# State-space block and routed feed-forward on one core: constants on another queue, loads reordered at the start, four more weight tiles resident before the last router logits

## Chip, core and metric

The kernel runs on one core of a Trainium2 chip, in one launch. The metric is the device time of that launch in microseconds. The engines are named as in the profile: PE (TensorE, matmul), PEld (its weight load), DVE (VectorE), ACT (ScalarE), POOL (GpSimd) and SP (SyncE, which here only issues DMAs). All arrays are float32.

## What is computed

Four batches of 1024 tokens with 1024 features go through two layers. The first is a selective state-space layer over a context of 512 features; the second is a feed-forward layer whose two experts per batch are picked by a router that looks at the whole normalised batch.

```python
def ssm(hidden, z, in_proj_w, conv_w, conv_b, x_proj_w, dt_proj_w, dt_proj_b, A_log, D):
    x = einsum('ed,bld->bel', in_proj_w, hidden)            # 512 -> 1024 channels
    u = silu(causal_conv4(x, conv_w) + conv_b)
    dt_lo, Bm, Cm = split(einsum('ke,bel->bkl', x_proj_w, u), (32, 16, 16))
    delta = softplus(einsum('er,brl->bel', dt_proj_w, dt_lo) + dt_proj_b)
    A = -exp(A_log)
    # for each token t:  state = state * exp(delta_t * A) + (delta_t * u_t) * B_t ;  y_t = state . C_t
    y = (scan(...) + D * u) * silu(z)
    return swapaxes(y, 1, 2)

x = x + ssm(ctx, layernorm(x), ...)

def ffn(x, switch_w, switch_b, w1, b1, w2, b2, w3, b3):      # x: layernorm(x)
    logits = x.reshape(b, -1) @ switch_w.T + switch_b        # 1024*1024 values against 8 experts
    gate, top = top_k(softmax(logits), 2)
    h = gelu(x_heads @ w1[top].T + b1[top])                  # 16 heads of 64
    o = sum_k gate_k * (h @ w2[top].T + b2[top])
    return (x + o) @ w3.T + b3

x = x + ffn(layernorm(x), ...)
```

## The kernel before

The work is written out by hand for each engine, with semaphores between them. The scan is cut into 64 blocks, `g` = 0 to 63: 4 batches, two halves of 512 tokens (`TH`), and 8 blocks of 128 channels (`J`). One block is one *step* and has 8 *slots*; a slot is a pair of the 16 states, for which ACT makes the decay `dA`, DVE the product with B (L1343) and two scans (L1370), POOL the product with C (L791), and PE the sum over states by transposing into `yT` (L854). The class `Schedule` says in which slot every other piece of work runs; each engine walks the same list `PLAN.slots[b][t]` in order. While batch `b` is scanned, the feed-forward layer of batch `b-1` runs between the scans. The last feed-forward has nothing beside it; it is the list of `b = 4`, made by `tail`.

**The start.** Before slot 0 each engine has a piece written out by hand.
- SP issues, in this order: the context (`ctxs`), the first block of in_proj weights, the convolution's `cw` and `cb`, then for `k` = 0 to 7 the weights of block `k` (into `Bb`, from `k` = 1 on) and the row block `k` of x (512 KB, into `Cb`), then the second half of the context (`first_ctx`, into `Bb[8:12]`), two more weight blocks (`win`) and `xz`. Then it waits for PE.
- ACT issues eleven small DMAs (L1029): five for the state-space layer (`Av`, `xpw`, two for `dtw`, `Dv`) and six for the feed-forward layer (`b1c` and `b2c` twice each, `b3c`, `swb`). All eleven count on one semaphore, `const_loaded`. Only behind them stands ACT's first work: for block `G` a copy of the last columns (L1040) and the first tap of the convolution (L1041), and, after DVE's three taps (L1218), Silu (L1056), which makes `u`.
- PE computes in_proj for `G` = 0 to 7 (L861, 8 matmuls a block in the trace), and behind block `G >= 2` the part of x_proj for block `G - 2` (L837). The first x_proj part waits for `const_loaded`, and PE runs its queue in order. Then come block 8, the last part of x_proj, the first delta (L846) and block 9.
- ACT's `split_rows` copies the result of x_proj out. SP stores the B and C rows to `bc_d` in DRAM and loads them back, spread over all partitions, one slot's pair `q` at a time into `Bb` and `Cb` (L542, 512 KB each). Ahead of the first of these it waits until in_proj of block 9 is done (`xin_done`), since `first_ctx` still lies in `Bb[8:12]`.
- DVE's block `G` is three taps and then the statistics of row block `G` (L1254 to L1260). After block 9's taps it makes the first product with B.

**The tail.** The router's logits of a batch's second half are 32 tiles of weights (`sw`, 512 KB each, four row blocks of 8) against normalised rows (L986). In the tail the tiles go through a ring of 19 places (`ring_t`): 3 in `sww`, 4 in `w3h`, 8 in `Cb` and 4 in `Bb`. The first 7 are loaded in slot 0 of the tail, in the last microseconds of the scan; the 12 in `Cb` and `Bb` after the last scan has let go of these; the last 13 are refills. Four row blocks for later (`Bb<-x_scratch`) are issued between the 12 and the 13. Behind the last logit come the router (L1306 to L1441), the experts and the output product (L1007, 16 output tiles), which occupy PE to the end.

`u` is a ring of 10 places (`UR`); block `g` uses place `g % 10`, so no block is written into it after block 63.

## Time and profile before

| | us |
|---|---|
| median of 3 runs | 2579.28 |
| lowest, highest | 2577.56, 2580.72 |
| the profiled execution | 2580.0 |
| its span, first to last instruction | 2578.2 |

| engine | busy us | share of the span |
|---|---|---|
| DVE | 2238.0 | 87% |
| PE | 1940.0 | 75% |
| ACT | 1537.1 | 60% |
| POOL | 1446.6 | 56% |

How to read it: the shares are averages over three different stretches. Between about 90 and 2350 us the scans run and DVE has almost no gap. Before 90 us stands the hand-written start, after 2350 us the last feed-forward. The page's line of 40 slices (64 us each) shows DVE at 3 tenths in the first slice and at 5, 2, 1 and 0 in the last four. The chain that ended last has 32% of the span on PE, 26% on DVE and 23% in issue.

### The profile page before, as it was taken

What the parts mean: (1) busy time and instruction counts of PE and PEld (TensorE: products, weight loads), DVE (VectorE), ACT (ScalarE), POOL (GpSimd) and SP (SyncE); (2) the same over time, 40 slices, a digit from 0 to 9 for tenths busy, and PEclk for the clock granted to TensorE, in tenths of its full rate; (3) what the DMA queues carried; (4) which work ended last, traced back from release to release, by engine and by line L of the source; (5) the groups of instructions that cost most, each with busy time, mean ns of one, the idle gap of its engine ahead of it and who ended that gap; (6) DMA issues with size and microseconds to landing.
All of it is one profiled execution on the core that took longest, in us unless ns stands there. A gap on an engine that the chain in (4) does not pass through costs nothing.

```text
span 2578.2 us, 30156 instructions
## 1 busy us (share of the span) xinstructions
PE 1940.0 (75%) x9488; PEld 1093.3 (42%) x9488; DVE 2238.0 (87%) x2928; ACT 1537.1 (60%) x2221; POOL 1446.6 (56%) x990
## 2 busy tenths in 40 slices
PE   5565656666776898898675888799685797896799
PEld 2344444344443454454443455344453354453244
DVE  3899999999999899998999989998999999995210
ACT  1566556555667657854666757855576858852400
POOL 0477666666775556665775656565775666663000
PEclk8767776887887899998787999999787999997899
DMA  5411252545552364566452364466460274566511
GB/s 150 164 33 57 83 172 76 178 147 176 194 174 100 98 216 147 158 207 200 170 206 74 116 229 139 141 215 197 159 235 21 72 238 147 175 193 226 211 57 66
DMA packets 201617, 387.84 MB, mean 150 GB/s; under 512 B 31697, under 2 KB 97233, under 8 KB 201458
## 3 DMA queue, kind: packets, MB, share of 16 engines
q1 hardware_dynamic: 194992, 385.43, 44.8%
q10 hardware_dynamic: 6466, 0.48, 0.2%
q8 instruction: 76, 1.25, 0.2%
q14 instruction: 83, 0.68, 0.1%
HBM read 351.78 MB, written 34.08 MB: 150 GB/s over the span
## 4 chain that ended last, share of the span: by engine, by line
PE 32%; DVE 26%; issue 23%; ACT 9%; POOL 6%; DMA 2%; SPq 1%; DVEq 1%; ACTq 1%; POOLq 0%
DVE h L1370 12%; PE dense L1007 10%; PE dense L854 7%; DVE dense L1343 5%; POOL h L791 5%; PE dense L825 4%; ACT dA L1127 3%; DVE u L1218 3%; PE dense L837 2%; PE dense L928 1%; PE dense L938 1%; ACT L1084 1%; PE dense L846 1%; DVE szT L1287 1%; PE dense L861 1%
## 5 line engine op out<-in xcount | busy, mean ns | idle before, releaser
L791 POOL TENSOR_TENSOR h<-h,Cb 128x1024 f32<-128x1024 f32 x512 | 1208.5, 2360 | 456.3 <-DVE h L1370 432.7
L1127 ACT ACTIVATE dA<-delta,Av 128x512 f32<-128x512 f32 x1024 | 702.6, 717 | 519.9 <-DVE h L1370 517.4
L854 PE MATMUL dense<-ident,h 128*128 128x128 f32 x4096 | 643.3, 313 | 289.6 <-POOL h L791 287.5
L854 PEld LDWEIGHTS dense<-ident,h 128*128 128x128 f32 x4096 | 550.9, 162 | 465.5 <-POOL h L791 376.8
L1370 DVE TENSOR_TENSOR_SCAN h<-dA,state,dense 128x512 f32<-128x512 f32 x512 | 627.6, 1263 | 41.3 <-PE dense L854 22.4
L1343 DVE TENSOR_TENSOR dense<-dense,Bb 128x512 f32<-128x512 f32 x1024 | 652.9, 683 | 5.0 <-DMA Cb<-bc_scratch 2.9
L1370 DVE TENSOR_TENSOR_SCAN h<-dA,dense 128x512 f32<-128x512 f32 x512 | 597.3, 1202 | 17.6 <-ACT dA L1127 9.9
L1007 PE MATMUL dense<-w3h,xT 128*128 128x512 f32 x832 | 390.5, 603 | 0.0
L785 POOL COPY state<-h 128x2 f32<-128x2 f32 x256 | 48.0, 187 | 373.3 <-DVE h L1370 371.8
L846 PE MATMUL dense<-dtaug,dtw 33*128 33x512 f32 x128 | 103.0, 896 | 180.0 <-DVE u L1218 178.2
L825 PE MATMUL dense<-ctxs,win 128*128 128x512 f32 x432 | 224.4, 667 | 1.9 <-ACT dtw L1063 1.0
L1007 PEld LDWEIGHTS dense<-w3h,xT 128*128 128x128 f32 x832 | 149.1, 194 | 129.6 <-issue 129.6
L1218 DVE SCALAR_TENSOR_TENSOR u<-dense,cw,u 128x511 f32<-128x511 f32 (+2 forms) x192 | 140.3, 731 | 35.8 <-ACT u L1041 28.0
L1084 ACT ACT_TABLE_LOAD x113 | 145.0, 1283 | 2.0
L1329 DVE TENSOR_TENSOR res<-dense,res 128x512 f32<-128x512 f32 x64 | 43.8, 684 | 111.3 <-PE dense L1007 110.9
L825 PEld LDWEIGHTS dense<-ctxs,win 128*128 128x128 f32 x432 | 90.9, 221 | 111.4 <-issue 111.4
L986 PE MATMUL dense<-sww,row 128*32 128x256 f32 x1336 | 110.9, 418 | 14.3 <-ACT row L1160 14.3
L1080 ACT COPY dense<-du_s 128x512 f32<-128x512 f32 x64 | 37.6, 588 | 134.2 <-DVE dense L1343 134.2
L846 PEld LDWEIGHTS dense<-dtaug,dtw 33*128 33x128 f32 x128 | 25.6, 249 | 211.3 <-issue 211.3
L938 PE MATMUL dense<-hs,w2s 128*64 128x512 f32 x224 | 71.3, 707 | 41.4 <-ACT hs L1192 40.6
L748 POOL TENSOR_TENSOR du_s<-delta,u 128x512 f32<-128x512 f32 x64 | 81.6, 1275 | 5.7 <-DVE delta L1248 5.7
L778 POOL TENSOR_TENSOR xt<-szT,xt 128x512 f32<-128x512 f32 x64 | 81.7, 1277 | 3.0 <-DVE szT L1287 3.0
(141 smaller groups left out, 1846.0 us busy)
## 6 DMA issues: line engine op xcount, KB each, us to landing
sww<-in_sw SPq DMA_DIRECT2D x170, 512.0 KB, 4.4
Bb<-bc_scratch SPq DMA_DIRECT2D x64, 512.0 KB, 4.6
Cb<-bc_scratch SPq DMA_DIRECT2D x64, 512.0 KB, 5.8
w3h<-in_sw SPq DMA_DIRECT2D x56, 512.0 KB, 7.6
w3h<-in_w3T SPq DMA_DIRECT2D x52, 512.0 KB, 5.1
row<-x_scratch SPq DMA_DIRECT2D x42, 512.0 KB, 4.8
xz<-in_x SPq DMA_DIRECT2D x64, 256.0 KB, 5.0
xt<-in_x SPq DMA_DIRECT2D x64, 256.0 KB, 4.4
```

What stands on the lines that cost most here:

```text
L791: e.tensor_tensor(h[:, s:s + 2, :], h[:, s:s + 2, :], Cb[:, 2 * q:2 * q + 2, :], ALU.mult).then_inc(prod_done, 1)
L825: mm = e.matmul(dense[:, bank, :], win[:, par, k, :], ctxs[:, k, :], start=(k == 0), stop=(k == DK - 1))
L846: e.matmul(dense[:, S, :], dtw[0:DR + 1, j * P:(j + 1) * P], dtaug[:], start=True, stop=True) \
L854: mm = e.matmul(yT[:, k, :], h[:, 2 * (q % RH) + i, k * P:(k + 1) * P], ident[:], is_transpose=True, start=False, stop=(q == PAIRS - 1 and ...
L938: mm = e.matmul(dense[HD * i:HD * i + HD, bank, :], w2s[:], hs_of(b, hp)[:, i, :], start=True, stop=True)
L986: mm = e.matmul(dense[32 * n:32 * n + 32, F2, 0:32 * E], rows[:, lo:lo + 32], weights[:, :, 32 * n:32 * n + 32], start=first, stop=(k % TB ...
L1007: mm = e.matmul(dense[:, bank, :], xT_of(b, uu)[:, d, k * P:(k + 1) * P], w3[:, d, :], start=False, stop=(d == J - 1), skip_group_check=True)
L1084: e.preload_act_table_set("natural_log_exp_and_others")
L1127: e.activation(dst, delta[:, st % 2, :], ACT.Exp, scale=Av[:, j * N + n:j * N + n + 1]).then_inc(dA_done, 1)
L1218: i = e.scalar_tensor_tensor(out=u[:, G % UR, s:T], in0=dense[:, bank, 0:T - s], scalar=cw[:, j, k:k + 1], in1=u[:, G % UR, s:T], op0=ALU. ...
L1343: e.tensor_tensor(duB[:, n % 2, :], du[:], Bb[:, n, :], ALU.mult).then_inc(duB_done, 1)
L1370: e.tensor_tensor_scan(h[:, 2 * (q % RH) + n % 2, :], decay, inflow, state[:, j * N + n:j * N + n + 1] if th else 0.0, ALU.mult, ALU.add) \
```

## The change

Four edits:
1. The six feed-forward constants leave ACT's queue. SP issues them behind `xz`, on a semaphore of their own, `ffn_const_loaded`. `const_loaded` counts five. DVE waits for the new semaphore at each `route1`, PE once, ahead of the first output tile of batch 1.
2. On SP the loads of in_proj weights go two places ahead of the row blocks of x.
3. The wait for block 9's in_proj stands ahead of the pair `q = 4` of the B/C loads, not ahead of `q = 0`.
4. The tail's ring has 23 places: four new ones at its head, in places 4 to 9 and 0 to 1 of `u`. They are loaded in slots 112, 114, 116 and 118 of the last batch, each behind waits for the blocks that used that place. 9 refills are left.

```diff
-RING_A, RING_B, RING_T = 8, 3, 19
+RING_A, RING_B, RING_U, RING_T = 8, 3, 4, 23
...
     def tail(self, rows):
         b = NB
-        for i in range(RING_T):
-            self.add(b, 0 if i < RING_B + 4 else 5, "sw_load", TB + i // SWL, i % SWL)
+        for i in range(RING_U):
+            self.add(b - 1, 112 + 2 * i, "sw_ahead", i)
+        for i in range(RING_U, RING_T):
+            self.add(b, 0 if i < RING_U + RING_B + 4 else 5, "sw_load", TB + i // SWL, i % SWL)
...
-        ring_t = [*ring_b, *sw_tiles(w3h[:], 4), *sw_tiles(Cb[:], 8), *sw_tiles(Bb[:, 8:16, :], 4)]
+        ring_t = [*sw_tiles(u[:, 4:UR, :], 3), *sw_tiles(u[:, 0:2, :], 1), *ring_b, *sw_tiles(w3h[:], 4), *sw_tiles(Cb[:], 8), *sw_tiles(Bb[:, 8:16, :], 4)]
...
-        CONSTS = 11
+        CONSTS, FFN_CONSTS = 5, 6
...
-            for k in range(J):
-                if k:
+            for k in range(J + 2):
+                if 0 < k < J:
                     e.dma_start(first_win[k], w_inT[k]).then_inc(first_win_loaded[k], 16)
+                if k < 2:
+                    continue
+                k -= 2
                 e.dma_start(first_rows[k], x[0:1, k * P:(k + 1) * P, :].rearrange("o p d -> p (o d)")) \
...
             load_xz(0, 0, 0)
+            with nc.allow_non_contiguous_dma(reason="small weights, once"):
+                for dst, src in (
+                    (b1c[0:HD], b1.rearrange("e f -> f e")),
...
+                    (swb[:], sw_b.partition_broadcast(P)),
+                ):
+                    e.dma_start(dst, src).then_inc(ffn_const_loaded, 16)
             e.wait_ge(xin_done, 1 + J + 1)
             load_ctx(0, 1)
...
             e.wait_ge(bc_stored, 1 + 16)
-            e.wait_ge(xin_done, 1 + 1 + AHEAD)
             for q in range(PAIRS):
+                if q == J // 2:
+                    e.wait_ge(xin_done, 1 + 1 + AHEAD)
                 e.wait_ge(first_row_read, 1 + q + 1)
                 load_bc(0, q)
...
+                    elif what == "sw_ahead":
+                        last = ALL - AHEAD + 2 * a[0] + 1
+                        e.wait_ge(uD_done, 1 + last + 1)
+                        e.wait_ge(du_s_done, 1 + last + 1)
+                        dst, done, _ = sw_tile(NB, TB, a[0])
+                        e.dma_start(dst, sw[TB * P:(TB + 1) * P, a[0]]).then_inc(done, 16)
...
                         if part == 0:
+                            if b == 1 and uu == 0 and dh == 0 and k == 0:
+                                e.wait_ge(ffn_const_loaded, 1 + 16 * FFN_CONSTS)
...
                     (Dv[:], D.rearrange("(j p) -> p j", p=P)),
-                    (b1c[0:HD], b1.rearrange("e f -> f e")),
-                    (b1c[HD:P], b1.rearrange("e f -> f e")),
-                    (b2c[0:HD], b2.rearrange("e d -> d e")),
-                    (b2c[HD:P], b2.rearrange("e d -> d e")),
-                    (b3c[:], b3.rearrange("(j p) -> p j", p=P)),
-                    (swb[:], sw_b.partition_broadcast(P)),
...
                 e.wait_ge(lg_done, 1 + b)
+                e.wait_ge(ffn_const_loaded, 1 + 16 * FFN_CONSTS)
```

ACT's queue at the start, before. Each row is an instruction with what it writes and reads; in brackets the semaphores it waits for.

```order
L1029 DMA Dv<-in_D 128x8x1
L1029 DMA b1c<-in_b 64x8x1 x2
L1029 DMA b2c<-in_b 64x8x1 x2
L1029 DMA b3c<-in_b 128x8x1
L1029 DMA swb<-in_sw_b 128x8
L1040 ACT_TABLE_LOAD [waits u_done,edge_done,xin_done]
L1040 COPY halo<-dense 128x3 [waits conv_loaded]
```

The same place after the change:

```order
L1050 DMA xpw<-in_x_projT 128x8x64
L1050 DMA dtw<-in_dt_projT 32x1024
L1050 DMA dtw<-in_dt_b 1x1024
L1050 DMA Dv<-in_D 128x8x1
L1061 ACT_TABLE_LOAD [waits u_done,edge_done,xin_done]
L1061 COPY halo<-dense 128x3 [waits conv_loaded]
```

The table load, which waits for block 0's in_proj, now stands right behind `Dv`.

SP's queue at the start, before, from `xz` to the first pairs of B and C:

```order
L546 DMA xz<-in_x 128x512
L537 DMA ctxs<-in_ctxT 128x4x512 [waits xin_done]
L566 DMA bc_scratch<-dtw 32x512 [waits evac0]
L542 DMA Bb<-bc_scratch 128x1024 [waits first_row_read,xin_done,bc_stored]
L542 DMA Cb<-bc_scratch 128x1024
L542 DMA Bb<-bc_scratch 128x1024 [waits first_row_read]
```

And after, to pair 4 (two rows for each of the pairs 1 to 3 left out):

```order
L549 DMA xz<-in_x 128x512
L578 DMA b1c<-in_b 64x8x1 x2
L578 DMA b2c<-in_b 64x8x1 x2
L578 DMA b3c<-in_b 128x8x1
L578 DMA swb<-in_sw_b 128x8
L540 DMA ctxs<-in_ctxT 128x4x512 [waits xin_done]
L582 DMA bc_scratch<-dtw 32x512 [waits evac0]
L545 DMA Bb<-bc_scratch 128x1024 [waits first_row_read,bc_stored]
L545 DMA Cb<-bc_scratch 128x1024
...
L545 DMA Bb<-bc_scratch 128x1024 [waits first_row_read,xin_done]
```

The six constants stand between `xz` and the second context load, and the wait for `xin_done` moved from the first pair to the fifth.

SP's queue in the tail, before:

```order
L588 DMA Bb<-x_scratch 128x1024 [waits x1_stored,duB_s_done,duB_done] x4
L669 DMA sww<-in_sw 128x1024 [waits sw_used] x3
L669 DMA w3h<-in_sw 128x1024 [waits sw_used] x4
L669 DMA Cb<-in_sw 128x1024 [waits sw_used] x6
L686 DMA w3h<-in_w3T 128x1024 [waits sw_used]
```

And after:

```order
L605 DMA Bb<-x_scratch 128x1024 [waits x1_stored,duB_s_done,duB_done] x4
L694 DMA u<-in_sw 128x1024 [waits sw_used] x4
L694 DMA sww<-in_sw 128x1024 [waits sw_used] x3
L694 DMA w3h<-in_sw 128x1024 [waits sw_used] x2
L711 DMA w3h<-in_w3T 128x1024 [waits sw_used]
```

The 13 refills have become 9, and the first four of them go into `u`.

## Rows read from the trace of the kernel before

**Rows 1.** The page, part 1: busy us, share of the span, instructions.
```profile
PE 1940.0 (75%) x9488; PEld 1093.3 (42%) x9488; DVE 2238.0 (87%) x2928; ACT 1537.1 (60%) x2221; POOL 1446.6 (56%) x990
```

**Rows 2.** Chain that ended at 110 us: start, us, what.
```profile
23.54 18.74 DMA swb<-in_sw_b
...
82.83 6.35 DMA Cb<-bc_scratch
```

**Rows 3.** Timeline of the start: start, us, engine, line, operation [idle before <-releaser].
```profile
14.81 2.85 ACTq L1029 DMA_DIRECT2D b1c<-in_b  x2
...
20.70 0.16 POOL L722 MEMSET cw<- 128x72 f32 x1 [10.01 <-DMA cb<-in_conv_b]
...
23.54 7.81 ACTq L1029 DMA_DIRECT2D swb<-in_sw_b  x1
...
30.15 1.20 SPq L546 DMA_DIRECT2D xz<-in_x  x1
31.52 1.28 ACT L1040 ACT_TABLE_LOAD   x1 [31.52 <-issue]
```

**Rows 4.** Timeline of PE and its weight loads at the start.
```profile
16.98 13.49 PE L861 MATMUL dense<-ctxs,Bb 128*128 128x512 f32 x24 [16.98 <-DMA Bb<-in_w_inT]
...
23.20 0.43 PEld L861 LDWEIGHTS dense<-ctxs,Bb 128*128 128x128 f32 x2 [0.63 <-DMA Bb<-in_w_inT]
...
42.32 1.97 PE L837 MATMUL dense<-u,xpw 128*64 128x512 f32 x2 [11.86 <-DMA swb<-in_sw_b]
...
49.12 1.07 PE L837 MATMUL dense<-u,xpw 128*64 128x512 f32 x2
...
69.52 3.70 PE L861 MATMUL dense<-Bb,win 128*128 128x512 f32 x8
```

**Rows 5.** Timeline of DVE at the start: taps, and the first product with B.
```profile
33.69 2.32 DVE L1218 SCALAR_TENSOR_TENSOR u<-dense,cw,u 128x511 f32<-128x511 f32 x3 [21.55 <-ACT u L1041]
...
37.74 2.31 DVE L1218 SCALAR_TENSOR_TENSOR u<-dense,cw,u 128x511 f32<-128x511 f32 x3
...
84.00 2.31 DVE L1218 SCALAR_TENSOR_TENSOR u<-dense,cw,u 128x511 f32<-128x511 f32 x3 [3.92 <-ACT u L1050]
89.20 1.30 DVE L1343 TENSOR_TENSOR dense<-dense,Bb 128x512 f32<-128x512 f32 x2 [2.88 <-DMA Cb<-bc_scratch]
```

**Rows 6.** DMA queues (q1 SP's, q10 ACT's), 0 to 22 us: packets, MB, share.
```profile
q1 hardware_dynamic: 3053, 2.20, 39.2%
q10 hardware_dynamic: 3690, 0.47, 17.4%
```

**Rows 7.** The same two queues, 0 to 36 us.
```profile
q1 hardware_dynamic: 4908, 7.36, 62.2%
q10 hardware_dynamic: 5494, 0.48, 13.8%
```

**Rows 8.** SP's store of B and C, timeline; landing times of their DMAs.
```profile
75.82 0.34 SPq L566 DMA_DIRECT2D bc_scratch<-dtw  x1
...
DMA to landing us min/median/max: 1.6/10.0/15.0
```

**Rows 9.** Stretches: from:to us, busy (count) by engine, PEclk, DMA share, GB/s.
```profile
2288.00:2320.00 32.00, 30.68 (x173) 16.63 (x174) 31.79 (x38) 18.69 (x27) 21.48 (x11) 1.00 0.65 200
2374.00:2390.00 16.00, 10.18 (x100) 3.67 (x96) 0.00 (x0) 2.20 (x4) 0.00 (x0) 0.79 1.03 409
```

**Rows 10.** Timeline of PE in the tail's logits.
```profile
2367.39 2.79 PE L986 MATMUL dense<-sww,row 128*32 128x256 f32 x24 [13.87 <-ACT row L1160]
...
2376.52 0.64 PE L986 MATMUL dense<-Cb,row 128*32 128x256 f32 x8 [0.64 <-DMA Cb<-in_sw]
...
2380.36 1.08 PE L986 MATMUL dense<-Cb,row 128*32 128x256 f32 x8 [0.20 <-DMA Cb<-in_sw]
...
2398.03 1.97 PE L915 MATMUL dense<-ident,ctxs 128*128 128x128 f32 x8
...
2407.22 0.64 PE L986 MATMUL dense<-Cb,ctxs 128*32 128x256 f32 x8 [0.60 <-DMA Cb<-in_sw]
```

More of the change, by code:

```diff
@@ L358, in build @@
         const_loaded = sem("const_loaded")
+        ffn_const_loaded = sem("ffn_const_loaded")
         first_win_loaded = [sem(f"first_win_loaded{G}") for G in range(J)]
@@ L562, in _ @@
             load_xz(0, 0, 0)
+            with nc.allow_non_contiguous_dma(reason="small weights, once"):
+                for dst, src in (
+                    (b1c[0:HD], b1.rearrange("e f -> f e")),
+                    (b1c[HD:P], b1.rearrange("e f -> f e")),
+                    (b2c[0:HD], b2.rearrange("e d -> d e")),
+                    (b2c[HD:P], b2.rearrange("e d -> d e")),
+                    (b3c[:], b3.rearrange("(j p) -> p j", p=P)),
+                    (swb[:], sw_b.partition_broadcast(P)),
+                ):
+                    e.dma_start(dst, src).then_inc(ffn_const_loaded, 16)
             e.wait_ge(xin_done, 1 + J + 1)
@@ L649, in slot @@
                         m = SWL * (k % TB) + i
-                        ring = RING_B if k < TB else RING_A if b < NB else RING_T
+                        if b == NB:
+                            m -= RING_U
+                        ring = RING_B if k < TB else RING_A if b < NB else RING_T - RING_U
                         if m >= ring:
-                            e.wait_ge(sw_used, 1 + sw_index(b, k, i) - ring + 1)
+                            e.wait_ge(sw_used, 1 + sw_index(b, k, i) - (RING_T if b == NB else ring) + 1)
                         elif k < TB:
```

## The prediction

> **What bounds the kernel now.** The page first: DVE is busy 87% of the span [rows 1], but that average says nothing of the two ends, where the change sits. So I read the start and the tail each by chain, timeline and DMA views.
>
> *The start.* The chain that ended at 110 us [rows 2] has one large piece: 18.74 us up to the landing of `swb`, a feed-forward constant that nobody needs before batch 1. The timeline of ACT says what else it does [rows 3]: the six feed-forward DMAs occupy ACT's queue from 14.81 to 31.35 us, and only then comes its first table load. PE [rows 4] has three in_proj blocks done at 16.98 + 13.49 = 30.47 us, then stands 11.86 us for `swb`, comes back slower (x_proj 1.97 us against 1.07 later) and ends block 8 at 73.22. DVE's first taps start at 33.69, and its first product at 89.20 waits 2.88 us for C [rows 5]. Two things are therefore late at once: ACT, which frees DVE, and the constants, which free PE.
>
> *The scans.* DVE is busy 31.79 of 32.00 us near the end of them [rows 9]. What the start gives arrives whole at the tail.
>
> *The tail.* DMA moves 409 GB/s at a share of 1.03 from 2374 to 2390 us, while PE is busy 10.18 of 16 us [rows 9]; ahead of a tile that takes 0.64 us it stands 0.64 us for the transfer, and so still at 2407.22 [rows 10]. The logits are bound by the volume of weights. Behind them runs a chain in which nothing can overtake.
>
> **The change, part by part.**
>
> *Constants off ACT.* After it ACT's next instruction is the table load that waits for in_proj of block 0. That block ends when block 1's weights are loaded, at 23.20 [rows 4]; `cw` and `cb` are there at 20.70 [rows 3]. The load starts at 23.2 instead of 31.52, 8.3 us earlier, and DVE's first taps at 33.69 - 8.3 = 25.4.
>
> PE's x_proj part 0 now wants five constants. By their shapes these are 3 x 1024 packets and under 200 for `dtw`, some 3,270; ACT's queue had moved 3,690 at 22 us [rows 6]. They are there 8 us before 30.47. It wants `u` of block 0 too: a whole DVE cycle is 37.74 - 33.69 = 4.05 us [rows 5], so 25.4 + 4.05 = 29.5 at the latest. PE goes on at 30.47 without a gap and without the slow restart. Then x_proj part 0 and block 3 take 1.07 + 3.70 less 0.1 of overlap, 4.7 us; from x_proj part 1 to the end of block 8 it was 73.22 - 49.12 = 24.1. End of block 8: 30.47 + 4.7 + 24.1 = 59.2 instead of 73.22, **14.0 us earlier**. Is DVE late instead? It reaches block 7's taps at 25.4 + 7 x 4.05 = 53.8; PE ends block 7 at 59.2 less 3.70 and two x_proj parts, 53.6, and ACT's step comes after that. PE stays the bound, with less than 1 us between them. All that follows block 8 up to the taps of block 9 is a fixed sequence: these end at 72.3 instead of 86.3.
>
> *Constants on SP.* SP is free at 31.35 [rows 3]. Even if the six issues take their 16.5 us again it is free at 47.9. Next on its queue is the second context load, released by block 7's in_proj at 53.6, then the store of B and C at 75.82 - 14.0 = 61.8 [rows 8]. Cost nothing; the cover is 5.7 us for the one and 13.9 for the other. The new waits (DVE at each `route1`, PE once) come hundreds of us later and are met: nothing, or some tens of ns each.
>
> *Weights before row blocks.* Block 1 waited 0.63 us ahead of its weight load, most of it the usual step from block to block: a gain of 0.1 at most, below nothing not, since row block 0 is wanted by DVE only at 25.4 + 2.3 = 27.7. The context, three weight blocks and that row block are 2.4 MB, and SP's queue had 2.20 MB over at 22 us; after that a row block and a weight block (0.79 MB) take 2.1 us at (7.36 - 2.20) MB in 14 us [rows 6, 7], against DVE's 4.05. Counted as 0.
>
> *B and C earlier.* The store is issued at 61.8; 1.6 us is the shortest landing of this stretch [rows 8], and the store goes into an idle queue: 63.4. The first C load is issued 0.4 us later and took 6.35 [rows 2]: 70.2. DVE's taps end at 72.3, so the C wait is gone and the conv is last: first product at **72.3 instead of 89.20, 16.9 us**. Without this edit the loads would begin behind block 9, as before, and the gain would stay at 14.0; it pays 2.9. Pair 4's wait ends with block 9, about 68.4; the four pairs before it are 4.2 MB, 10 us at 409 GB/s, so DMA has work until 73.6. Bounds: a landing of 10.0 us, the median [rows 8], gives 73.8 and 15.4 in all, one of 15.0 gives 78.8 and 10.4. I take 6.35, the same transfer into the same empty queues, and 13 for the low end.
>
> *Four tiles ahead.* A tile is 524,288 bytes, 1.28 us at 409 GB/s; four fewer in the bound stretch: **5.1 us**. The refills are released by tiles 0 to 8, which PE has done long before. The ahead loads go into 2288 to 2320 us, where DMA runs at 200 GB/s and share 0.65 [rows 9]: 2.1 MB more make 266. Nothing there waits for a load, so I cost them at nothing; without that cover they could cost up to 5.1. The other bound is PE at its low clock: a tile then takes 1.08 us, 1.01 net, and a turn of a row block 1.9 [rows 10]. Tile 30 would start at 2367.39 + 30 x 1.01 + 3 x 1.9 = 2403.4 instead of 2402.1 by DMA, and the last pieces cost another 1.3: a gain of 2.5. I take 5.1, since PE keeps up at 1.28 us a tile at either clock; above, 5.5.
>
> The rows speak against a rule here. Tiles come every 1.28 us, because transfers overlap. The Trainium skill (DMA: Bandwidth & Descriptors, the table of fixed and variable time ahead of "Queues, rings and completion order") puts about 2.0 us fixed on every DMA beside bytes / 436e9; by it four tiles would be worth 4 x 3.2 = 12.8 us. The trace does not agree.
>
> *Sum.* 16.9 + 5.1 = 22.0 us. The profiled execution took 2580.0 (1.8 outside its span), 0.7 above the median; a shift is the same for both: 2558.0 for such an execution, 2579.28 - 22.0 = **2557.3** for the median.
>
> **The rivals.**
> 1. *The start pays less*: B and C, or the five constants, land later than counted. For it: landings of 10 to 15 us exist in this stretch. Against it: those were queued behind others. With 13 at the start: 2561.2.
> 2. *The tail pays nothing or half*: the ahead loads push the steps' own, or PE's clock stays low. 2562.4 with nothing, 2559.9 with 2.5.
> 3. *The tiles pay more than volume*, each with its own latency, 1.6 + 1.28 = 2.9 us, 11.5 for four: 2550.9. Only if they went one at a time, which 409 GB/s excludes. The skill's fixed cost named above would be this case.
> 4. *PE still waits* behind a constant that lands late for another reason, and ACT's release buys nothing: 2.9 + 5.1 = 8.0, 2571.3.
> 5. *Slower: the six constants block SP.* Their issue stalls on SP, and behind it stand the context load and the store of B and C. Each us that SP is free after 61.8 + 2.1 = 63.9 costs one; from 85.9 on, 54.5 us for the six, the whole gain is gone; with 60 us it is 2584.8. Against it: they took 16.5 us on ACT, and in the time that they waited their packets moved one for one with SP's (1,804 and 1,855 between 22 and 36 us [rows 6, 7]). Behind x they have no such neighbour: 3,200 packets at the 562 per us of 10 to 22 us are 5.7 us. The one-for-one is what the Trainium skill says (the same page, "Queues, rings and completion order": each engine takes turns between queues packet by packet); by that rule the trace agrees, and this rival is the weaker for it.
>
> **How the numbers follow.** Chances: forecast 0.69, first rival 0.13, second 0.10, third 0.01, fourth 0.03, fifth 0.02, and 0.02 that both ends fail and the time stays. The range takes in the first two rivals and the bounds: low 2579.3 - 17.1 - 5.5 = 2556.7, less 1.7 for the spread of the runs shown, 2555.0; high 2579.3 - 13 - 2.5 = 2563.8. A measurement of this kernel can tell 0.2%, 5.2 us, from no change: faster 0.96, same 0.02, slower 0.02.
>
> **What the profile after would show.** ACT's first table load near 23.2 and DVE's first taps near 25.4; no gap in PE between block 2 and x_proj part 0, and both parts of it near 1.07; block 8 ending near 59.2; DVE's first product near 72.3 with ACT or its own taps, not C, ahead of it; SP's six issues over before 53.6. In the tail `u<-in_sw` loads between 2270 and 2300, 409 GB/s again in the logits, and from their first to their last 5.1 us less. Wrong would be: a DMA wait ahead of x_proj part 0, pair 0 landing after 72.3, a DVE gap where the ahead loads go, or PE busy through the logits.

## The result and the profile after

| | before | changed |
|---|---|---|
| median us (6 runs each, side by side) | 2579.20 | 2560.52 |
| lowest, highest | 2577.56, 2580.72 | 2559.50, 2563.02 |
| ratio, 95% interval | | 0.9929 [0.9917, 0.9942] |
| the profiled execution, its span | 2580.0, 2578.2 | 2559.85, 2557.8 |

18.7 us faster, where 22.0 were forecast and the range allowed 15.5 to 24.3. I cut both traces at five landmarks to see where the time came from:

| stretch, us | before | changed | gain | forecast |
|---|---|---|---|---|
| start of span to the first product with B | 89.20 | 72.47 | 16.7 | 16.9 |
| to the end of the last scan | 2259.87 | 2260.61 | -0.7 | 0 |
| to the first router logit of the tail | 18.32 | 18.56 | -0.2 | 0 |
| first to last logit | 42.06 | 37.44 | 4.6 | 5.1 |
| to the end | 168.75 | 168.72 | 0.0 | 0 |

The gains sum to 20.4 us of span. Outside the span the changed kernel takes 0.2 us more (2.05 instead of 1.8). The medians are 1.5 us closer together than the two profiled executions, of which the one before lies 0.8 above its median and the one after 0.7 below.

**The start.** Timeline of the changed kernel, ACT and SP, as [rows 3] (start, us, engine, line, operation, in brackets idle before and its releaser; a q is the engine's DMA issuing):

```profile
29.93 1.78 SPq L578 DMA_DIRECT2D b1c<-in_b  x2
31.76 7.06 SPq L578 DMA_DIRECT2D b2c<-in_b  x2
38.86 1.53 SPq L578 DMA_DIRECT2D b3c<-in_b  x1
40.43 0.58 SPq L578 DMA_DIRECT2D swb<-in_sw_b  x1
53.99 0.38 SPq L540 DMA_DIRECT2D ctxs<-in_ctxT  x1
62.06 0.34 SPq L582 DMA_DIRECT2D bc_scratch<-dtw  x1
63.70 0.34 SPq L545 DMA_DIRECT2D Bb<-bc_scratch  x1
...
24.00 1.28 ACT L1061 ACT_TABLE_LOAD   x1 [24.00 <-PE dense L886]
```

ACT's table load now waits for PE, not for its own issues. SP takes 11.1 us for the six constants and is free 13 us before the next thing is due. PE and DVE, as [rows 4, 5]:

```profile
17.48 13.32 PE L886 MATMUL dense<-ctxs,Bb 128*128 128x512 f32 x24 [17.48 <-DMA Bb<-in_w_inT]
30.72 1.07 PE L862 MATMUL dense<-u,xpw 128*64 128x512 f32 x2
...
55.75 3.70 PE L886 MATMUL dense<-Bb,win 128*128 128x512 f32 x8
63.20 5.40 PE L886 MATMUL dense<-Bb,win 128*128 128x512 f32 x8
...
26.17 2.31 DVE L1239 SCALAR_TENSOR_TENSOR u<-dense,cw,u 128x511 f32<-128x511 f32 x3 [13.77 <-ACT u L1062]
70.24 2.32 DVE L1239 SCALAR_TENSOR_TENSOR u<-dense,cw,u 128x511 f32<-128x511 f32 x3 [3.92 <-ACT u L1071]
72.47 1.29 DVE L1364 TENSOR_TENSOR dense<-dense,Bb 128x512 f32<-128x512 f32 x2
```

The 11.86 us that PE stood for `swb` are gone and x_proj part 0 takes 1.07 us. Block 8 ends at 55.75 + 3.70 = 59.45. The first product has no bracket: C was there. The page's part 3 gives the queues (packets, MB, share):

```profile
q10 hardware_dynamic: 3170, 0.47, 0.1%
```

3170 packets are what ACT's five constants alone make; the estimate by shapes was 3,270.

**The tail.** SP's ahead loads:

```profile
2272.15 0.33 SPq L669 DMA_DIRECT2D u<-in_sw  x1
2280.03 0.40 SPq L669 DMA_DIRECT2D u<-in_sw  x1
2286.67 0.39 SPq L669 DMA_DIRECT2D u<-in_sw  x1
2292.74 0.45 SPq L669 DMA_DIRECT2D u<-in_sw  x1
```

Two stretches, columns as in [rows 9]:

```profile
2271.00:2303.00 32.00, 30.23 (x167) 15.87 (x166) 31.79 (x37) 18.96 (x27) 22.24 (x11) 1.00 0.83 277
2374.00:2390.00 16.00, 12.36 (x86) 4.20 (x84) 0.81 (x2) 5.02 (x7) 0.00 (x0) 0.55 0.70 278
```

The first is the stretch of [rows 9] moved with the scans: 277 GB/s instead of 200 (266 forecast), and DVE's 31.79 us of 32 are the same. From 2360 to 2376 us, in the logits, DMA moved 409 GB/s as before. The second stretch catches the end of the logits, where the last transfers run out; its granted clock of 0.55 means that PE ran nearly all of it at 1.2 GHz. PE's rows there, as [rows 10]. L1011 is the tiles, eight matmuls each; L940 x8 is a *turn*, eight transposes of a normalised row block between two groups of tiles:

```profile
2351.64 3.26 PE L1011 MATMUL dense<-u,row 128*32 128x256 f32 x32 [14.12 <-ACT row L1181]
...
2373.29 1.94 PE L940 MATMUL dense<-ident,ctxs 128*128 128x128 f32 x8 [2.04 <-ACT xT L1202]
...
2385.52 1.08 PE L1011 MATMUL dense<-w3h,ctxs 128*32 128x256 f32 x8 [0.19 <-DMA w3h<-in_sw]
2386.53 1.97 PE L940 MATMUL dense<-ident,ctxs 128*128 128x128 f32 x8
2388.43 0.65 PE L1011 MATMUL dense<-w3h,ctxs 128*32 128x256 f32 x8
```

The tile at 2385.52 is the last but one, and still waits for its transfer. Its start lies 21.7 us before the same tile's 2407.22 [rows 10], more than the 20.4 that remain at the end. So the transfers gave more than the sum shows, and PE took some back behind them: tile and turn cost 1.08 and 1.97 us here, where the kernel before had 0.64 and 1.09 in the same place.

### The profile page after: what moved, and what is told of

It reads as the page before. It is cut to its first block, busy times and chain, and to the rows that moved or that the text cites. A ratio compares the mean times of both kernels' runs of the same rounds, so it can differ in the third digit from the quotient of the medians.

```text
span 2557.8 us, 30169 instructions
## 1 busy us (share of the span) xinstructions
PE 1942.7 (76%) x9488; PEld 1096.3 (43%) x9488; DVE 2238.3 (88%) x2928; ACT 1537.2 (60%) x2221; POOL 1445.2 (57%) x990
## 3 DMA queue, kind: packets, MB, share of 16 engines
q10 hardware_dynamic: 3170, 0.47, 0.1%
## 4 chain that ended last, share of the span: by engine, by line
PE 35%; DVE 26%; issue 22%; ACT 9%; POOL 5%; DMA 2%; DVEq 1%; SPq 0%; ACTq 0%; POOLq 0%
DVE h L1391 12%; PE dense L1034 11%; PE dense L879 7%; DVE dense L1364 5%; POOL h L816 5%; PE dense L850 4%; ACT dA L1148 3%; DVE u L1239 3%; PE dense L862 2%; PE dense L963 2%; PE dense L953 2%; PE dense L886 2%; PE dense L1011 1%; ACT L1105 1%; DVE szT L1308 1%
## 5 line engine op out<-in xcount | busy, mean ns | idle before, releaser
L879 PE MATMUL dense<-ident,h 128*128 128x128 f32 x4096 | 647.4, 314 | 282.4 <-POOL h L816 280.1
L879 PEld LDWEIGHTS dense<-ident,h 128*128 128x128 f32 x4096 | 554.1, 163 | 459.1 <-POOL h L816 368.5
L1391 DVE TENSOR_TENSOR_SCAN h<-dA,dense 128x512 f32<-128x512 f32 x512 | 597.7, 1204 | 17.5 <-ACT dA L1148 9.8
L850 PE MATMUL dense<-ctxs,win 128*128 128x512 f32 x432 | 223.4, 665 | 1.9 <-ACT dtw L1084 1.0
L1239 DVE SCALAR_TENSOR_TENSOR u<-dense,cw,u 128x511 f32<-128x511 f32 (+2 forms) x192 | 140.6, 732 | 21.7 <-ACT u L1062 13.8
L850 PEld LDWEIGHTS dense<-ctxs,win 128*128 128x128 f32 x432 | 90.4, 220 | 110.8 <-issue 110.8
L1011 PE MATMUL dense<-sww,row 128*32 128x256 f32 x1336 | 109.8, 415 | 0.4 <-ACT row L1181 0.4
L963 PE MATMUL dense<-hs,w2s 128*64 128x512 f32 x224 | 72.3, 717 | 41.4 <-ACT hs L1213 40.6
```

The lines of the kernel that those rows point to most:

```text
L850: mm = e.matmul(dense[:, bank, :], win[:, par, k, :], ctxs[:, k, :], start=(k == 0), stop=(k == DK - 1))
L879: mm = e.matmul(yT[:, k, :], h[:, 2 * (q % RH) + i, k * P:(k + 1) * P], ident[:], is_transpose=True, start=False, stop=(q == PAIRS - 1 and ...
L963: mm = e.matmul(dense[HD * i:HD * i + HD, bank, :], w2s[:], hs_of(b, hp)[:, i, :], start=True, stop=True)
L1011: mm = e.matmul(dense[32 * n:32 * n + 32, F2, 0:32 * E], rows[:, lo:lo + 32], weights[:, :, 32 * n:32 * n + 32], start=first, stop=(k % TB ...
L1239: i = e.scalar_tensor_tensor(out=u[:, G % UR, s:T], in0=dense[:, bank, 0:T - s], scalar=cw[:, j, k:k + 1], in1=u[:, G % UR, s:T], op0=ALU. ...
L1391: e.tensor_tensor_scan(h[:, 2 * (q % RH) + n % 2, :], decay, inflow, state[:, j * N + n:j * N + n + 1] if th else 0.0, ALU.mult, ALU.add) \
```

## Experiments

Three theories stood at the start. **A**, the prediction: start and tail pay separately, the start through ACT and PE together, the tail by DMA volume. **B**: one of the two releases at the start does it all and the other is idle change. **C**: what is missing from 22.0 is lost to something the change adds (ahead loads, or loads in another order). Gains below are of medians, against the kernel before in the same series.

### Constants off ACT alone

```diff
-        CONSTS = 11
+        CONSTS, FFN_CONSTS = 5, 6
...
             load_xz(0, 0, 0)
+            (the six feed-forward constants, on ffn_const_loaded)
             e.wait_ge(xin_done, 1 + J + 1)
```

> The kernel before with edit 1 alone: the six feed-forward constants on SP behind xz, on a semaphore of their own. The theory of the prediction: PE's gap of 11.86 us ahead of x_proj part 0 and its slow restart go, block 8 ends 14.0 us earlier, and since B and C are still loaded only behind block 9 the first product keeps its wait for C of about 2.9 us: first product at about 75.2, and the run 14.0 us faster than before. Rival (SP's queue becomes the bound): the store of B and C is issued later than 61.8 and the gain is smaller by that.

Measured: 2567.41 (2566.67 to 2569.92), ratio 0.9952 [0.9936, 0.9969], a gain of 13.0. Block 8 ended at 58.40, but the first product stood at 72.56, earlier than expected. PE and DVE rows of this kernel:

```profile
17.14 5.08 PE L872 MATMUL dense<-ctxs,Bb 128*128 128x512 f32 x8 [17.14 <-DMA Bb<-in_w_inT]
...
72.56 1.30 DVE L1350 TENSOR_TENSOR dense<-dense,Bb 128x512 f32<-128x512 f32 x2 [2.75 <-DMA Cb<-bc_scratch]
```

The wait for C is back (2.75 us), as theory A says; the start is early mostly because block 9's in_proj took 3.70 us here, against 5.40 in the changed kernel. Of the 16.6 us that the start gave in this trace, 12.5 are left in the span: 1.0 went in the scans and 2.1 in the logits (44.14 us instead of 42.06), 1.2 behind them.

### The wait for block 9 alone

```diff
-            e.wait_ge(xin_done, 1 + 1 + AHEAD)
             for q in range(PAIRS):
+                if q == J // 2:
+                    e.wait_ge(xin_done, 1 + 1 + AHEAD)
```

> The kernel before with edit 3 alone: the wait for block 9's in_proj stands ahead of pair 4 of the B and C loads. Theory: the loads start about 5 us earlier, the first product follows DVE's taps of block 9 directly, at about 86.3 instead of 89.2, and the run is 2.9 us faster. Rival (landing is slower with other traffic about): C is still waited for, gain below 2 us.

Measured: 2577.39, ratio 0.9991 [0.9981, 1.0001] over 10 runs, a gain of 3.0; the interval touches no change. The trace shows the place: SP loads B at once behind the store, and the product has lost its wait and starts 2.98 us before the 89.20 of [rows 5].

```profile
77.45 0.34 SPq L542 DMA_DIRECT2D Bb<-bc_scratch  x1
...
86.22 1.28 DVE L1344 TENSOR_TENSOR dense<-dense,Bb 128x512 f32<-128x512 f32 x2
```

### The ring of 23 places alone

```diff
-RING_A, RING_B, RING_T = 8, 3, 19
+RING_A, RING_B, RING_U, RING_T = 8, 3, 4, 23
...
+            self.add(b - 1, 112 + 2 * i, "sw_ahead", i)
```

> The kernel before with edit 4 alone: 23 places in the tail's ring, four tiles loaded during the last scans. Theory A, volume: the logits' last transfer is 5.1 us earlier. Theory B, volume and clock: the same transfer gain, but PE, which is busier between transfers, ends the stretch at its low clock, so that the last turn of a row block and the last tile take about 1.3 us more: 3.8 to 4.6 us faster. Rival: the ahead loads disturb the scans, seen as DVE gaps in the last two steps that the kernel before has not, and the gain is 0 to 3.

Measured: 2575.57, ratio 0.9979 [0.9969, 0.9988] over 10 runs, a gain of 4.8. The stretch of [rows 9] in this kernel:

```profile
2288.00:2320.00 32.00, 30.82 (x177) 16.77 (x175) 31.79 (x38) 18.37 (x27) 21.66 (x11) 1.00 0.78 262
```

DVE's 31.79 us are untouched and the scans took 2260.09 us against 2259.87: the ahead loads are free, which leaves theory C only the order of loads. Of this trace's gain 0.9 us stand at the start, which the edit does not touch (first product at 88.31), and 3.5 in the logits (38.61 us against 42.06). The last tile but one started 4.8 us earlier after the last scan, and PE took 1.3 back behind it: the expectation's theory B. The three parts alone sum to 13.0 + 3.0 + 4.8 = 20.8 us. The whole, measured twice, gave 18.7 and 20.7.

### PE released, ACT not

The six constants stay on ACT's queue, behind the five, on a semaphore of their own.

```diff
                     e.dma_start(dst, src).then_inc(const_loaded, 16)
+                for dst, src in (
+                    (the same six)
+                ):
+                    e.dma_start(dst, src).then_inc(ffn_const_loaded, 16)
```

> The kernel before with only the semaphore split: the six feed-forward constants stay on ACT's queue, but PE's x_proj part 0 waits for five constants only. ACT is as late as before (first table load near 31.5), PE is not held by the last constant. If both lateness were the same thing, this gives all 14 us. By my reading the bound passes to ACT and DVE: taps start at 33.7 and come every 4.05 us, so u of block 6 is ready near 61.0, block 8 ends near 65.7 instead of 73.2, and the run is about 7.5 us faster than before.

Measured: 2575.35 (2571.08 to 2580.02, 10 runs), ratio 0.9983 [0.9974, 0.9993], a gain of 5.0. Expected were 7.5. In the trace the first product came 10.3 us earlier, up to 3.1 of them without the edit: ACT's issues ended at 28.39, not at 31.52.

```profile
21.13 7.08 ACTq L1035 DMA_DIRECT2D swb<-in_sw_b  x1
28.39 1.28 ACT L1046 ACT_TABLE_LOAD   x1 [28.39 <-issue]
...
33.68 1.04 PE L838 MATMUL dense<-u,xpw 128*64 128x512 f32 x2 [3.07 <-ACT u L1062]
```

PE now waits for ACT's `u` instead of for `swb`. With ACT at 31.52, as before, 7.2 would be left. The tail gave 3.5 back: logits 44.19 (before 42.06), the rest 170.17 (before 168.75).

### ACT released, PE not

The kernel with the constants off ACT alone, in which PE's x_proj part 0 waits for all eleven constants again.

```diff
                     e.wait_ge(const_loaded, 1 + 16 * CONSTS)
+                    e.wait_ge(ffn_const_loaded, 1 + 16 * FFN_CONSTS)
                     e.wait_ge(evac[S], 1 + 1)
```

> Edit 1 on the kernel before, but PE's x_proj part 0 waits for all eleven constants again, six of which now come over SP's queue behind xz. ACT is free early (first table load near 23), PE waits. By my reading PE is what ends the start: it goes on when the last of the six lands, 43 to 46 us against 42.3 before, and the run is 1 to 4 us slower than the kernel before, although DVE has its taps of blocks 0 to 2 done 8 us earlier. If instead ACT's release carried part of the 14 us by itself, this is faster than before.

Measured: 2581.21, ratio 1.0004 [0.9995, 1.0014]: no gain, and the 1 to 4 us of loss that were expected are not clear of the interval either.

```profile
43.67 1.94 PE L848 MATMUL dense<-u,xpw 128*64 128x512 f32 x2 [13.39 <-issue]
...
25.65 2.32 DVE L1226 SCALAR_TENSOR_TENSOR u<-dense,cw,u 128x511 f32<-128x511 f32 x3 [13.44 <-ACT u L1049]
```

DVE starts its taps 8.0 us earlier than in [rows 5] and then waits for PE (the wait is put down to issue; behind it stands the semaphore that I added). Against theory B: ACT's release alone is worth nothing, PE's alone 5.0, both together 13.0. Each was the other's cover.

### Row blocks before weights

The changed kernel with the old order of loads.

```diff
-            for k in range(J + 2):
-                if 0 < k < J:
+            for k in range(J):
+                if k:
                     e.dma_start(first_win[k], w_inT[k]).then_inc(first_win_loaded[k], 16)
-                if k < 2:
-                    continue
-                k -= 2
```

> The changed kernel without edit 2: weights and row blocks of x alternate on SP's queue as before. Theory: edit 2 is worth nothing that can be measured: DVE's first product within 0.3 us of the changed kernel's 72.5, the same total. Rival: without it block 1 or 2 waits for its weights (up to 1 us), or with it PE's first matmul comes later (17.48 against 16.98 us), so that this one is up to 0.5 us faster.

Measured: 2561.77 (2560.60 to 2564.44), ratio 0.9926 [0.9910, 0.9943]. The change itself had 0.9929 [0.9917, 0.9942]: edit 2 cannot be told from nothing. In its trace the first product came at 70.04, 2.4 us before the 72.47 of the changed kernel, since block 9's in_proj took 3.70 us, and then the scans took 2265.52 us against 2260.61. The 2.4 us were given back twice over. That spread had to be understood before a difference of a few us meant anything.

One rival stays open. In all seven traces of kernels with edit 2, block 9's in_proj took 5.31 to 5.40 us and the first product came at 71.50 to 72.47 (71.29 and 71.39 with PE kept busy at the start). In the two traces with an early start and without edit 2 (this one and constants off ACT alone) it took 3.70 us, and DVE's taps of block 9 ended at 70.12 and 69.80. So edit 2 may cost these 1.7 us at the start through PE's clock. Against it: three kernels with the late start took 5.40 us without edit 2 too, and the medians show no loss.

### The changed kernel once more

> The changed kernel once more, beside the other three of this job, as their base, and for a second trace of it. The three differ from it by 1 to 6 us, and runs of one kernel lie up to 3.5 us apart. Theory: the spread comes from PE's granted clock falling or rising at other places in the scans and the tail, so that the second trace has the same start to within 0.3 us after PE's first matmul, and loses or gains 1 to 3 us in steps where PE is slower in one trace than in the other.

Measured: 2560.05 (2556.81 to 2565.46), ratio 0.9912 [0.9897, 0.9927], a gain of 20.7. The profiled execution happened to be the longest, 2565.46, and is worth more than a typical one: it is the same code as the first trace and its span is 5.6 us longer. The scans took 4.7 more (2265.28 against 2260.61) and the part behind the logits 1.9 more, while the first product came 1.0 earlier (71.50). Both expectations were too narrow: 0.3 us for the start, 1 to 3 for the rest. I laid the two DVE timelines over each other and looked for the instructions at which the distance jumps. The largest jump is 2.0 us. The next in size within the scans (1.2 up, 1.2 down, 0.9 up) also stand at a DVE wait for PE, as does one of 1.9 behind the logits. First trace:

```profile
2013.08 1.91 PE L879 MATMUL dense<-ident,h 128*128 128x128 f32 x16
...
2028.94 1.08 PE L963 MATMUL dense<-hs,w2s 128*64 128x512 f32 x4 [0.20 <-issue]
...
2030.06 0.75 DVE L1342 SCALAR_TENSOR_TENSOR xT<-dense,b2s,xT 128x512 f32<-128x512 f32 x1 [0.66 <-PE dense L963]
```

The same place in the second:

```profile
2014.68 3.54 PE L879 MATMUL dense<-ident,h 128*128 128x128 f32 x16
...
2028.36 4.83 PE L862 MATMUL dense<-u,xpw 128*64 128x512 f32 x7 [1.32 <-ACT szT L1172]
...
2034.54 0.75 DVE L1342 SCALAR_TENSOR_TENSOR xT<-dense,b2s,xT 128x512 f32<-128x512 f32 x1 [2.65 <-PE dense L963]
```

The same 16 transposes take 1.91 and 3.54 us, x_proj (L862) comes later and slower, L963 behind it ends late, and DVE waits 2.65 us instead of 0.66. The granted clock was 0.68 from 2008 to 2016 us in the first trace and 0.50 from 2010 to 2018 in the second. At 103 us it is the same with a smaller stake: eight matmuls of L850 took 4.33 us in the first trace and 5.58 in the second, and a scan waited 0.58 us for L879. PE's mean granted clock over 90 to 250 us was even higher in the second trace, 0.72 against 0.67. What counted in these two traces was not how much of the time PE is slow, but whether it is slow in the few us in which DVE needs it. Why the clock falls at one place in one execution and at another in the next, these runs do not show.

The Trainium skill (TensorE: Matmul & The Clock Gate, "What's actually happening") says of a kernel's start that the number of matmuls at the low clock differs from run to run. The traces agree: block 0's eight matmuls took 6.45 us in the first trace of the changed kernel and 5.53 in the second.

### Two tiles ahead instead of four

```diff
-RING_A, RING_B, RING_U, RING_T = 8, 3, 4, 23
+RING_A, RING_B, RING_U, RING_T = 8, 3, 2, 21
```

> The changed kernel with two tiles loaded ahead into u (places 4 to 7), not four; 21 places and 11 refills. If the tail's gain is volume, 1.28 us a tile, this is 2.6 us slower than the changed kernel, all of it between the first and the last logit. If the gain came from something else (the first tiles being there at all, or PE's clock), it is 0 to 1 us slower.

Measured: 2563.66 (2559.33 to 2565.61), ratio 0.9928 [0.9915, 0.9942], 3.6 above the changed kernel in the same series, with intervals that touch. In the trace the logits took 38.25 us, only 0.8 more than 37.44. The last tiles show why that length misleads:

```profile
2387.07 0.64 PE L1011 MATMUL dense<-Cb,ctxs 128*32 128x256 f32 x8 [0.61 <-DMA Cb<-in_sw]
2387.64 1.09 PE L940 MATMUL dense<-ident,ctxs 128*128 128x128 f32 x8
2388.66 0.64 PE L1011 MATMUL dense<-Cb,ctxs 128*32 128x256 f32 x8
```

Here PE was at 2.4 GHz and the last turn took 1.09 us, in the changed kernel 1.97. The volume is read at the start of the last tile but one, counted from the end of the last scan, which releases the last places of the ring:

| kernels | tiles ahead | last tile but one, us after the last scan |
|---|---|---|
| before; constants off ACT; block 9's wait; PE freed; ACT freed | 0 | 58.15; 58.57; 58.33; 58.41; 57.81 |
| two tiles | 2 | 54.77 |
| changed, twice; ring alone; rows first; PE busy at the start | 4 | 52.44, 52.03; 53.37; 52.87; 52.87 |

The means are 58.25, 54.77 and 52.72: 5.5 us for four tiles (5.1 counted), 3.5 for the two (2.6). The kernel of the next section, the same tail with filler, has 51.93. Two tiles lie between none and four, and each is worth 1.4 to 1.7 us. That is more than the 1.28 of its volume, but kernels with the same tail differ by 0.8 us (none ahead) and 1.3 us (four ahead), so the excess is not shown.

### Filler for PE between the last tiles

Two transposes of `ident` into a PSUM bank that nobody reads then, behind each of the tiles 23 to 30. They are added work; the output is the same.

```diff
                         mm.then_inc(sw_used, 1)
+                        if b == NB and 23 <= SWL * (k % TB) + i <= 30:
+                            ...
+                            for _ in range(2):
+                                e.transpose(dense[:, YT, 0:P], ident[:], ident[:])
```

> The changed kernel, with two 128x128 transposes of the identity into an unused PSUM bank behind each of the router's tiles 23 to 30 in the tail, as filler that only keeps PE busy. Theory, clock: PE's turn of the last row block takes about 1.1 us instead of 1.97 and the last logit comes 0.9 to 1.3 us earlier; the rest of the tail the same. Rival, no clock effect: the tiles stay at 1.08 us and PE falls behind by up to 0.2 us a tile, so that this is 0 to 1.6 us slower.

Measured: 2559.85 (2557.54 to 2561.76), ratio 0.9919 [0.9903, 0.9936]: not separable from the changed kernel. PE's rows:

```profile
2386.49 0.64 PE L1011 MATMUL dense<-w3h,ctxs 128*32 128x256 f32 x8 [0.24 <-DMA w3h<-in_sw]
...
2387.34 1.04 PE L940 MATMUL dense<-ident,ctxs 128*128 128x128 f32 x8
2388.30 0.64 PE L1011 MATMUL dense<-w3h,ctxs 128*32 128x256 f32 x8
```

The last turn is 1.04 instead of 1.97 us, and the logits are 36.11 instead of 37.44 us, 1.3 less, as much as the low clock takes from tile and turn. What follows the logits took 0.3 us more. That the filler did it is not shown by this one trace. The kernel with PE kept busy at the start (below) has no filler in the tail, and its trace has the last tiles at 0.64 us, the turn at 1.09 and the logits at 36.07 us.

### The experts' weights later

In the tail SP loads the experts' weights ahead of the ring's 12 tiles. They move behind them.

```diff
-        self.add(b, 4, "experts")
+        self.add(b, 20, "experts")
```

> The changed kernel, with the tail's four loads of expert weights (0.5 MB in runs of 256 bytes) issued behind the refills of the ring, not ahead of the 12 tiles. Theory, the logits are bound by what DMA has to move before the last tile: the stretch gets shorter by 1.3 us (bytes at 409 GB/s) to 2.6 us (289 GB/s were moved while these loads ran), and the experts land before the router needs them. Rival: the stretch is bound elsewhere (PE or the issue of SP) and nothing moves.

Measured: 2558.35 (2557.03 to 2559.59), ratio 0.9916 [0.9899, 0.9932], 1.5 below the filler in the same series. The last tile but one came 49.91 us after the last scan, 2.5 earlier than 52.44 and 2.0 earlier than the earliest of the traces with the experts ahead (51.93); the kernel with all three edits below has 49.29. The logits took 35.04 us. The stretch in which these loads were, in the changed kernel and then without them:

```profile
2344.00:2352.00 8.00, 0.36 (x4) 0.20 (x8) 4.22 (x12) 1.24 (x1) 1.48 (x4) 0.50 1.09 316
```

```profile
2344.00:2352.00 8.00, 0.52 (x8) 0.29 (x12) 4.38 (x12) 1.37 (x2) 1.47 (x4) 0.50 1.02 404
```

The DMA engines are fully busy in both, and move 316 and 404 GB/s. The experts' rows are 64 floats, 256 bytes. The Trainium skill (DMA: Bandwidth & Descriptors, "Specifications") wants runs of at least 512 bytes for the full rate; the two rows agree.

### PE kept busy before the first weights land

24 transposes of `ident`, added work again, ahead of block 0.

```diff
+            for _ in range(24):
+                e.transpose(dense[:, YT, 0:P], ident[:], ident[:])
             e.wait_ge(ctx_loaded, 1 + 16)
```

> The changed kernel with 24 transposes of the identity on PE while it waits for the context and the first weights. Theory: the start is one PE chain from its first matmul to the first product, and PE goes through its first block at 0.85 us a matmul against 0.43 later; started at the higher clock, block 0 takes 3.5 us instead of 6.2, and every landmark up to the first product comes 2.0 to 2.7 us earlier. Rivals: DMA ends the start (weights of block 1 are not there before 20.5), then 0 to 1 us; or DVE, which has less than 1 us to PE's chain, then about 1.

Measured: 2562.44 (2558.31 to 2563.68), ratio 0.9923 [0.9909, 0.9936]: no gain. The filler ended too early and PE stood again:

```profile
11.00 4.41 PE L898 MATMUL dense<-ident 128*128 128x128 f32 x24 [11.00 <-POOL ident L736]
17.38 12.23 PE L886 MATMUL dense<-ctxs,Bb 128*128 128x512 f32 x24 [1.96 <-DMA Bb<-in_w_inT]
```

12.23 us for the first three blocks is less than the 13.32 of the changed kernel's first trace, but in its second, without filler, they took 12.40. The experiment decides nothing on the clock at the start.

### All three together

The last three edits on top of the changed kernel.

> The changed kernel with all three at once: PE warmed at the start, experts issued behind the refills, filler between the last tiles. If the three add up: 2.5 + 2.4 + 1.3 = 6 us faster than the changed kernel, some 2554 to 2555. With the experts late the refills come without a break and PE has less idle time, so that filler may be worth nothing: then 4.5 to 5.

Measured: 2558.82 (2553.34 to 2558.96), ratio 0.9904 [0.9889, 0.9919], a gain of 21.9 over the kernel before. It has the lowest ratio, the fastest run and the shortest logits (33.82 us); the median of the kernel with the experts later, 2558.35, is lower, in another series. From the changed kernel in the same series, 2560.05, it is 1.2 away, and the intervals overlap: faster than before is shown, faster than the change is not. The 4.5 to 6 us that were expected did not come. Its logits gained 3.7 us over those of the changed kernel's second trace (37.50), the start 0.1.

## Why the prediction was right, point by point

- *ACT's table load at 23.2.* Measured 24.00, and 22.28 to 23.76 in other kernels without the six issues. I took block 0 to end when block 1's weights come; it ends when its own eight matmuls are done, 5.06 to 6.45 us after 17.1 to 17.5, depending on PE's clock. It costs nothing, since DVE is not the bound yet.
- *PE without a gap, block 8 at 59.2.* 59.45. Right, and the two half experiments show that both releases were needed. The fourth rival (PE still waits) is the kernel in which only ACT is freed; ACT's release bought nothing there, as that rival said; but the case did not come, since the five constants were there in time.
- *SP's cover.* Free at 41.0 (forecast 47.9 at most), next due at 53.99 (53.6), store at 62.06 (61.8). The slower case, SP blocked, would have needed 54 us for the six; it took 11.1.
- *Edit 3 pays 2.9, first product at 72.3.* 72.47 without a wait; alone 2.98 in the trace. The second trace of the same kernel has 71.50, so a hit to 0.2 us is partly luck.
- *Edit 2 counted 0.* Its removal gave 0.9926 against 0.9929. Nothing measurable, with an uncertainty of some 5 us; that it could not cost anything, as I wrote, is not shown, and block 9's 3.70 us in both early-start traces without it speak against that.
- *"What the start gives arrives whole at the tail."* This is the step that was too simple. DVE was busy 31.79 of 32.00 us in the stretch that I read, but over the whole scans it sometimes waits for PE, and how often differs between executions of one kernel: 2260.61 and 2265.28 us. In the first trace the change lost 0.7 us there. In the eight traces of the changed kernel and its variants the scans took 2260.3 to 2265.5 us, all of them above the 2259.87 of the kernel before; in the five of kernels with a part of the change, 2259.5 to 2263.6. The sum should have had a term of 0.4 to 5.6 us of loss for it. Whether the earlier start itself costs the scans something, or the trace of the kernel before is merely a short one, is not shown.
- *The tail pays 5.1.* The term was mis-sized in two ways that nearly cancel. Transfers gave 5.7 in the traces compared, 58.15 less 52.44. PE's low clock took 1.3 back behind the last transfer: turn and last tiles are the only pieces that no transfer hides. That is usual with four tiles ahead and not certain: from the start of the last tile but one to that of the last it was 2.9 us in five of the six such traces without filler and 1.59 in the sixth, and 1.59 to 2.68 without tiles ahead. I had both numbers, and put the second only into the low bound (2.5), as if the tail were bound either by DMA or by PE's clock. It is bound by DMA up to the last tile but one and by PE from there. The third rival (a fixed latency for each tile, 11.5) is excluded by 5.5 for four.
- *Ahead loads cost nothing.* Right: 262 and 277 GB/s with DVE at 31.79 us.
- *The sum.* 22.0 forecast, 20.4 in the span of the profiled executions: 0.2 missing at the start, 0.7 in the scans, 0.2 ahead of the logits, 0.5 in the logits (with rounding). The medians say 18.7 and in a second series 20.7. The 1.5 us between the first median and its trace are the places of the two profiled executions beside their medians; the 2.0 between the series are of the size by which two executions of one kernel differ in the scans, and a cause of its own for them was not found. The whole forecast is 3.3 and 1.3 us too high.

## What to carry to other kernels

When two engines wait at the start for different things that hang on the same queue, free both: PE's release alone gave 5.0 us, ACT's alone nothing, both 13.0. In a stretch bound by transfers, count the bytes moved out of it at the measured rate, and add what the last consumers cost once no transfer hides them, at the clock that they are granted then. Before a difference of a few us is explained, lay two executions of the same kernel over each other; the spread between them is the smallest effect that a single trace can show.

## What was not expected of the hardware

- PE's low clock falls at different places in two executions of the same program, and 16 transposes (1.91 or 3.54 us) in the wrong place cost DVE 2 us of the 4.7 by which the scans differ, 2260.61 and 2265.28 us.
- The time for issuing the same small DMA is no property of it: `swb` took 7.81 us on ACT's queue [rows 3], 7.08 in another kernel and 0.58 on SP's; `b2c`'s two took 2.37 us on ACT's queue and 7.06 on SP's.
- Loads in rows of 256 bytes in a saturated stream cost more than their 0.5 MB: the rate fell from 404 to 316 GB/s, and moving them behind the tiles brought the last tiles 2.5 us forward.
- PE's clock among the last tiles does not follow from the waits alone. In the kernel before, the tile at 2407.22 [rows 10] took 0.64 us behind 0.60 us of waiting; in the changed kernel, once PE had stood 2.04 us for ACT and 1.34 for a tile, each took 1.08 behind 0.2, up to the end. In the kernel with PE kept busy at the start it had stood as long, 2.47 us for ACT and 2.17 for a tile, and came back to 0.64 three tiles before the last but one; with two extra transposes a tile it came back too.
